# The causal mask of a fused four-layer attention kernel: on the four row tiles, 32 keys at a time, in place of products over the whole array

## The reference, cut to what matters

```python
scores = jnp.einsum('bhtd,bhsd->bhts', q, k) * q.shape[-1] ** (-0.5)
if causal:
    t, s = (scores.shape[-2], scores.shape[-1])
    mask = jnp.tril(jnp.ones((t, s), bool))
    scores = jnp.where(mask, scores, -jnp.inf)
p = jax.nn.softmax(scores, axis=-1)
o = jnp.einsum('bhts,bhsd->bhtd', p, v)
```

## Time and profile before

| | |
|---|---|
| time, median of 3 runs | 1405.27 us (1403.87 to 1406.78) |
| profiled execution: time, span | 1402.28 us, 1399.7 us |
| granted TensorE clock, mean | 0.996 of full |
| PE busy | 1343.6 us, 96% |
| PE weight loads (PEld) busy | 1144.9 us, 82% |
| DVE, ACT, POOL busy | 71%, 64%, 43% |

### The profile page before, as it was taken

The page is one execution under the profiler, slowest core; times in us unless marked ns, Lnnn a source line. Parts: engine busy times, 40 slices in busy tenths (PEclk is TensorE's granted clock), DMA queues, the critical chain, the costliest instruction groups (busy, mean ns, idle before and its releaser), DMA issues.

```text
span 1399.7 us, 45003 instructions
## 1 busy us (share of the span) xinstructions
PE 1343.6 (96%) x19500; PEld 1144.9 (82%) x19500; DVE 989.0 (71%) x1844; ACT 897.7 (64%) x1519; POOL 600.0 (43%) x767
## 2 busy tenths in 40 slices
PE   5899999999999999999999999999999999899997
PEld 5788888777887887787778888887999999688885
DVE  4777777787887777667766788788464445677675
ACT  4777677777767665666556776776443335767764
POOL 6644444676454732443334332225486665111100
PEclk9999999999999999999999999999999999999999
DMA  7211000101000100000000010000000000001000
GB/s 282 68 40 34 28 16 9 39 24 46 9 9 9 33 2 2 3 2 2 3 2 20 21 47 10 15 10 24 9 9 1 1 1 8 17 32 31 24 25 32
DMA packets 16316, 34.95 MB, mean 25 GB/s; under 512 B 1911, under 2 KB 7159, under 8 KB 15607
## 3 DMA queue, kind: packets, MB, share of 16 engines
q1 hardware_dynamic: 16119, 32.09, 7.2%
HBM read 27.89 MB, written 4.19 MB: 23 GB/s over the span
## 4 chain that ended last, share of the span: by engine, by line
PE 71%; DVE 14%; ACT 10%; issue 3%; DMA 1%; POOL 1%; SPq 0%; DVEq 0%; ACTq 0%; POOLq 0%
PE ps L712 9%; DVE s_nm L1098 9%; PE ps L777 8%; PE ps L739 6%; PE ps L805 6%; PE ps L791 6%; PE ps L657 5%; PE ps L604 5%; PE ps L756 5%; PE ps L629 4%; PE ps L616 4%; ACT s_PU L947 3%; PE ps L717 2%; PE ps L593 2%; PE ps L766 2%
## 5 line engine op out<-in xcount | busy, mean ns | idle before, releaser
L1098 DVE TENSOR_REDUCE s_nm<-ps 128x8 fp32r<-128x960 f32 (+1 forms) x352 | 395.5, 1167 | 108.6 <-PE ps L657 61.3
L947 ACT ACTIVATE s_PU<-ps 120x1024 f32<-120x1024 f32 (+1 forms) x288 | 279.5, 1025 | 103.8 <-PE ps L717 103.0
L712 PE MATMUL ps<-s_Qs,s_KH 32*120 32x256 f32 (+2 forms) x4608 | 184.4, 288 | 6.2 <-DVE s_nm L1098 2.9
L1222 POOL TENSOR_TENSOR s_xs<-s_xs,s_rowv 128x512 f32<-128x512 f32 x96 | 123.9, 1291 | 142.5 <-ACT s_nt L852 130.4
L1251 POOL TENSOR_SCALAR s_rs<-s_mv 128x2 f32<-128x2 f32 x96 | 21.7, 226 | 370.8 <-DVE s_mv L1135 364.9
L712 PEld LDWEIGHTS ps<-s_Qs,s_KH 32*120 32x120 f32 (+1 forms) x4608 | 150.6, 180 | 28.7 <-DVE s_nm L1098 6.1
L956 ACT ACTIVATE s_Os<-ps 128x512 f32<-128x512 f32 x160 | 94.5, 599 | 103.0 <-PE ps L739 55.8
L777 PE MATMUL ps<-s_W,s_oT 128*128 128x256 f32 x960 | 134.1, 289 | 3.5 <-DVE s_oT L1027 2.6
L604 PE MATMUL ps<-s_xT,s_W 128*128 128x256 f32 x960 | 135.3, 291 | 2.1 <-DVE s_xs L1119 1.4
L739 PE MATMUL ps<-s_PU,s_Vp 120*32 120x256 f32 x2048 | 129.1, 384 | 8.4 <-ACT s_PU L947 7.1
L777 PEld LDWEIGHTS ps<-s_W,s_oT 128*128 128x128 f32 x960 | 118.8, 188 | 13.9 <-issue 4.3
(11 more groups left out here) (100 smaller groups left out, 2592.4 us busy)
## 6 DMA issues: line engine op xcount, KB each, us to landing
s_cf<-ctx_t SPq DMA_DIRECT2D x32, 240.0 KB, 2.6
s_ws<-weights SPq DMA_DIRECT2D x28, 256.0 KB, 2.7
s_nt<-x_t SPq DMA_DIRECT2D x16, 256.0 KB, 2.8
s_xs<-x_nat SPq DMA_DIRECT2D x4, 1024.0 KB, 8.9
out<-s_xs SPq DMA_DIRECT2D x16, 256.0 KB, 2.0
s_rowv<-rows SPq DMA_DIRECT2D x6, 512.0 KB, 3.7
s_mi<-mask SPq DMA_DIRECT2D x8, 120.0 KB, 3.4
s_cst<-consts SPq DMA_DIRECT2D x1, 153.0 KB, 2.3
```

The lines of the kernel that those rows point to most:

```text
L712: e.matmul(banks[j][0:n, wide * x:wide * x + wide], kz[row[j], lk, g, c, k0:k0 + n], q[row[j], lq, g, qs_], start=(x == 0 and y_ == 0), st ...
L947: t = e.activation(P_of(i, k)[0:n, :, :], pair("B", i, k)[0:n, :, :], ACT.Exp, scale=0.25)
L1098: e.tensor_reduce(o, v, AX.X, ALU.max, negate=True).then_inc(sem["max"])
L1222: e.tensor_tensor(xs[:, b, :, :], xs[:, b, :, :], row2(layer, 0), ALU.add).then_inc(sem["pool"])
```

## The change

Each mask product over the whole array becomes four on every row tile, one for each block k of 32 queries. The stationary operand `who` (32x128, bf16) has ones that pick, for the queries of block k, the row of `gone` with the query's number in the block, and for the queries of earlier blocks the row 31, in which all is -2^100; `gone` (32x32, bf16, the same in each row tile) is the triangle of one block. The product is added on the 32 keys of block k, for all heads of the bank at once: 128 columns in unit 0 (four heads' slots of 32), 64 columns in units 1 and 2. So a unit has 16 mask matmuls in place of four, and `A` stays on the row tiles to its end.

`who` (128 KB) and `gone` (8 KB) are made on the host and come by two more DMAs in `mcols`; the constants are 64 KB smaller, and the two casts on DVE go. The plan is told that `A` of SELF ends on row tiles and takes 1.07 (before: 1.76 for unit 0 and 1.27 for the others). `STAY` goes from 0.006 to 0.236, and every entry of `WANT` but a few has another value, so that the order of all engines in all layers is another.

```diff
-WANT = dict(Xl=2.33, xT=-3, cT=-4, mi=-4, bo=(-1.38, -4.6, 0.82, 0.54, 4.02, -2.73), N=(0, 0, 7.36, 5.95, 4.46, 10.15),
+WANT = dict(Xl=-8.6, xT=-3, cT=-4, mi=-4, bo=(-0.05, 0.32, 4.13, 3.45, 8.95, -1.6), N=(0, 0, 6.16, 6.96, 8.36, 7.97),
...
+ROWMASK = True
 TURN = .19
-STAY = 0.006
+STAY = 0.236
...
-                array[0] = "whole" if name == "A" and layer_of(s.key[1]) == "SELF" else ARRAY.get(name, "whole")
+                array[0] = ARRAY.get(name, "whole")
...
-                    long=(1.76 if not u else 1.27) if self_ else .78 if layer == "L0" else None)
+                    long=1.07 if self_ else .78 if layer == "L0" else None)
...
-                w.wait_ge(sem["cst"], 4)
+                w.wait_ge(sem["d_msk"], 32)
...
-                    for j in range(4):
-                        t = e.matmul(banks[j].rearrange("p (r n) -> p r n", r=4), idb[:, :],
-                                     cbf[:, :].rearrange("p (o n) -> p o n", o=1).to_broadcast([128, 4, 128]), start=False, stop=True)
+                    off = [banks[j].rearrange("p (r b n) -> p r b n", r=4, b=4) for j in range(4)]
...
+                    off = [banks[j].rearrange("p (r b n) -> p r b n", r=2, b=8)[:, :, 4:8, :] for j in range(4)]
+
+                many = off[0].shape[1]
+                for k in range(4):
                     for j in range(4):
-                        t = e.matmul(banks[j].rearrange("p (c n) -> p c n", c=2)[:, :, 128:256], idb[:, :],
-                                     cbf[:, :].rearrange("p (o n) -> p o n", o=1).to_broadcast([128, 2, 128]), start=False, stop=True)
+                        t = e.matmul(off[j][:, :, k, :], who[row[j], k, :],
+                                     gone[row[j], :].rearrange("p (o n) -> p o n", o=1).to_broadcast([32, many, 32]),
+                                     start=False, stop=(k == 3))
                 t.then_inc(sem["A"])
...
-            e.tensor_copy(idb[:, :], ident[:, :]).then_inc(sem["cst"])
-            e.tensor_copy(cbf[:, :], caus[:, :]).then_inc(sem["cst"])
...
                 e.dma_start(mci[0:C, :], mask_t).then_inc(sem["d_mci"], 16)
+                e.dma_start(who[:, :, :].bitcast(u16), who_d).then_inc(sem["d_msk"], 16)
+                e.dma_start(gone[:, :].bitcast(u16), gone_d).then_inc(sem["d_msk"], 16)
...
+    q, row = np.arange(128)[None, None, :], part[:, None, None] % 32
+    block = np.arange(4)[None, :, None]
+    who = np.where(q // 32 == block, (row == q % 32) & (row < 31), (q // 32 < block) & (row == 31))
+    gone = np.where((np.arange(32)[None, :] > part[:, None] % 32) | (part[:, None] % 32 == 31), GONE, 0.0)
```

More of the change, by code:

```diff
@@ new lines @@
+WANT = dict(Xl=-8.6, xT=-3, cT=-4, mi=-4, bo=(-0.05, 0.32, 4.13, 3.45, 8.95, -1.6), N=(0, 0, 6.16, 6.96, 8.36, 7.97),
+            T=(0, -0.95, -0.09, -0.31, 0.05, -0.48), Q=(0.77, 0.4, 0.84, 0.53, 0, 0.96), Qh=(6.09, 3.57, 0.73, 1.06, 0, 0.55),
+            Ql=(4.86, 7.59, 5.47, 2.75, 0, 3.71), K=(0.69, 0.53, -0.61, -0.04, 0, 0.09), Kh=(8.28, 3.8, 10.87, 8.11, 0, 8.93),
+            Kl=(7.75, 11.88, 2.29, 5.3, 0, 6.15), K0=(-8.86, 4.8, 2.49, -0.38, 0, -5.31), V=(0.93, 1.19, 1.13, 1.09, 0, 1.14),
+            Ve=(6.09, 5.67, 5.17, 8.12, 0, 6.03), mf=5.42, A=(1.09, -0.04, -1.09, 0.86, 0, -0.96),
+            max=(0.19, -9.37, -4.86, -7.18, 0, 0.65), M=(-6.77, -4.88, -4.21, -4.16, 0, -9.54),
+            mTe=(5.28, 8.54, -0.91, -2.06, 0, 3.39), B=(-4.67, -7.08, -5.25, -3.98, 0, -6.3), exp=(-1.56, 3.06, 2.22, 3.8, 0, 4.84),
+            cap=-1.45, PV=(2.35, 1.54, 1.22, 1.96, 0, 2.46), PVe=(-4.89, -5.42, -3.15, 1.91, 0, 2.33),
+            ON=(3.22, 2.87, 3, 2.88, 0, -1.81), ONe=(1.73, 1.71, -1.22, -2.11, 0, 0.18), OT=(4.46, -4.46, 2.98, 2.5, 0, 3.93),
+            O=(-6.79, -9.94, -6.15, -1.26, 0, -4.83), y=(7.48, -1.3, 2.52, 6.31, 3.13, 1.93), st=(4.63, 7.35, 19.25, 15.89, 13.59, 0),
+            rs=(9.21, 4.54, 6.56, -2.53, 5.72, 0), ln=(5.45, 3.79, 0, 0, 0, 0), lng=(-7.5, -10.65, 0, 0, 0, 0), F1=-4.56, Fa=-4.54,
+            Fv=12.57, Hl=-14.14, F2=2.89, out=2.2, Th=(-5.93, -10.66, -3.47, -3.26, -7.11, -13.03),
+            Tl=(0, -1.48, 2.6, -2.01, 0.53, 4.69), OTh=(-7.18, -5.54, -13.03, -4.94, 0, -2.05),
+            OTl=(-4.46, 2.01, -4.88, -2.27, 0, -1.06), Ch=(5.54, 1.77, 0, -3.93, 0, -3.44), Cl=(-9.01, -5.12, 0, -5.24, 0, -7.35))
@@ L402, with program @@
 POOL_SEMS = ["pool"]
-DMA_SEMS = (["d_cst", "d_mci", "d_out"] + [f"d_x{k}" for k in range(4)] + [f"d_{n}{s}" for n in ("row", "mi", "nt") for s in range(2)]
+DMA_SEMS = (["d_cst", "d_mci", "d_msk", "d_out"] + [f"d_x{k}" for k in range(4)] + [f"d_{n}{s}" for n in ("row", "mi", "nt") for s in range(2)]
             + ["d_cf0"] + [f"d_ws{s}" for s in range(2)])
 N_CST = 16
-def program(nc, x_nat, x_t, ctx_t, mask, mask_t, weights, consts, rows, out):
+def program(nc, x_nat, x_t, ctx_t, mask, mask_t, weights, consts, who_d, gone_d, rows, out):
     f32, f32r, bf16, i32 = mybir.dt.float32, mybir.dt.float32r, mybir.dt.bfloat16, mybir.dt.int32
+    u16 = mybir.dt.uint16
     ALU, ACT, AX = mybir.AluOpType, mybir.ActivationFunctionType, mybir.AxisListType
@@ L444, in program @@
         rowv = [sb(f"rowv{i}", [128, 4, D]) for i in range(2)]
-        idb = sb("idb", [128, 128], bf16)
+        who = sb("who", [128, 4, 128], bf16)
         onb = sb("onb", [128, 128], bf16)
-        cbf = sb("cbf", [128, 128], bf16)
+        gone = sb("gone", [128, 32], bf16)
         pickr = sb("pickr", [128, 4], f32r)
@@ L450, in program @@
         gq = sb("gq", [128, 16])
-        cst = sb("cst", [128, 306])
-        ident, caus, hsel, pick, colv, c2 = (cst[:, a:b] for a, b in ((0, 128), (128, 256), (256, 258), (258, 262), (262, 282), (282, 306)))
+        cst = sb("cst", [128, 178])
+        ident, hsel, pick, colv, c2 = (cst[:, a:b] for a, b in ((0, 128), (128, 130), (130, 134), (134, 154), (154, 178)))
         ps = st.enter_context(nc.psum_tensor("ps", [128, 8, 512], f32))
@@ L641, in A @@
                 if layer == "L0":
-                    w.wait_ge(sem["cst"], 4)
+                    w.wait_ge(sem["cst"], 2)
                     w.wait_ge(sem["mf"], nth("mf", first))
@@ L943, in exp @@
                 if layer_of(i) == "L0":
-                    w.wait_ge(sem["cst"], 5)
+                    w.wait_ge(sem["cst"], 3)
                     t = e.activation(P_of(i, k)[0:n, :, :], pair("B", i, k)[0:n, :, :], ACT.Exp, scale=0.25, bias=mcol[0:n, i:i + 1])
@@ L1398, with bf16_bits @@
     part = np.arange(128)
-    causal = np.where(part[None, :] > part[:, None], GONE, 0.0).astype(np.float32)
+    q, row = np.arange(128)[None, None, :], part[:, None, None] % 32
+    block = np.arange(4)[None, :, None]
+    who = np.where(q // 32 == block, (row == q % 32) & (row < 31), (q // 32 < block) & (row == 31))
+    gone = np.where((np.arange(32)[None, :] > part[:, None] % 32) | (part[:, None] % 32 == 31), GONE, 0.0)
+    def bf16_bits(v):
+        return (np.ascontiguousarray(v, dtype=np.float32).view(np.uint32) >> 16).astype(np.uint16)
     headsel = np.stack([(part // 16) % 2 == 0, (part // 16) % 2 == 1], 1).astype(np.float32)
@@ L1406 @@
         "mask": g["mask_BxS2_if1"].reshape(B // 2, 2 * C), "mask_t": g["mask_BxS2_if1"].T,
-        "weights": weights, "consts": np.concatenate([np.eye(128, dtype=np.float32), causal, headsel, pick, cols], 1), "rows": rows,
+        "weights": weights, "consts": np.concatenate([np.eye(128, dtype=np.float32), headsel, pick, cols], 1),
+        "who": bf16_bits(who), "gone": bf16_bits(gone), "rows": rows,
     }
```

## The result

The changed kernel took 1396.39 us, the median of four runs (1395.82 to 1397.33), beside 1405.54 for the kernel before. The ratio is 0.9936, with a 95% interval of 0.9919 to 0.9954: 9.0 us faster, between 6.5 and 11.4. Measured again later on another chip it was 0.9957 (0.9945 to 0.9970), which is 6.4 us. The forecast was 1389.6 us with a range of 1377 to 1402. So the direction and the range were right, and the gain was forecast at 15.7 us, well above what came.

A forecast was written before the change was run, and what follows sets the result against it. The prediction took PE's instructions to bound an item of SELF. From 1405.27 us it took 13.1 us for the causal layer and 2.6 for the new order, 15.7 in all, with the start at 0: 1389.6 us, range 1377 to 1402.

The forecast's parts named there:

- The layer's 13.1 us: Causal layer SELF: net gain of 0.82 us for each of 16 items, 13.1 us in all.
- What goes: Per SELF item on PE: old mask products 2.09 us plus a weight-load stand of 0.21, 2.30 us removed.
- The 0.97 and twice 0.56: Old mask products per SELF item: 0.97 us for 512 columns, 0.56 each for units 1 and 2.
- What comes: Per SELF item on PE: 48 new row-tile matmuls add 1.32 us, bounded by 0.48 and 1.56.
- my lower bounds: New mask matmuls on row tiles: at least 15 ns with 128 columns and 7.6 ns with 64.
- the turn of 0.16 before `K`: After unit 0 in SELF: the turn to whole-array K is moved, not saved, adding 0.16 us per item.
- Rival (A): SELF: DVE's path takes over, wait for OTl grows 0.34 us, layer gains only 7.7 us; 1395.0 us, chance 0.17.
- The new order's 2.6 us: All layers: new due times and STAY save a quarter of a turn per attention item, 2.6 us.
- The start at 0: Kernel start: the two new mask DMAs cost 0, or 0.9 us if the assumed cover is gone.
- (B): Attention items: one turn fewer each, 10.4 us in place of 2.6; 1381.8 us, chance 0.17.
- (C): SELF: small matmuls cost 45 ns each and gain nothing, only the new order is left; 1402.7 us, chance 0.08.
- (D): Attention items outside SELF: passing over due stages starves PE, 28.8 us lost; 1421.0 us, chance 0.08.

The follow-up runs named there:

- The whole-array products in unit 2: Changed kernel with unit 2's mask added by 16 products of 64 columns over the whole array: 1397.50 us, 0.9956 of the kernel before.
- the doubling there: Changed kernel with the 16 mask products of unit 2 issued twice: 1396.37 us, 0.9946 of the kernel before.
- The products alone: New mask products with the order of the kernel before: 1395.33 us, 0.9940 of the kernel before.
- The kernel with both edits in the old order: New mask products in the old order, OTl ahead of Kl on DVE in SELF, mask DMAs behind the loads of x: 1389.45 us, 0.9902.
- the kernel with `OTl` first: New mask products in the old order, with OTl ahead of Kl on DVE: 1391.51 us, 0.9915 of the kernel before.
- the doubling in unit 1: Changed kernel with the 16 mask products of unit 1 issued twice: 1398.18 us, 0.9959 of the kernel before.

## Why the prediction was right in its range and too high in its gain

**The layer's 13.1 us** measured 16 x 0.76 = 12.2, but by errors that nearly cancel. *What goes* was too high by 0.21: the stand of the weight loads was counted beside distances from end to end, and unit 1 got shorter by 0.38 us, not by 0.60. The 0.97 and twice 0.56 stand. *What comes* was mis-sized the other way: by ends the 48 products add 0.25 + 2 x 0.17 = 0.59 us where I had 1.32. The line that I drew from 256 to 128 columns and on to 64 came from f32 rows. With bf16, 128 columns go at 0.25/16 = 15.6 ns where the f32 ones went at 28.8, and 64 columns at 8 ns: both are my lower bounds (15 and 7.6). The f32 weight load of 177 ns against 98 fits as the reason, and I named it and then set it aside; but the streamed operand changes its type too, and no run parts the two.

The page that I weighed, TensorEngine Tiling (Array Packing) of the Trainium skill, section Instruction Overhead, gives a matmul about 60 cycles of overhead, by my estimate 25 ns at 2.4 GHz. Read as a distance between any two matmuls, this doesn't hold here: the measurement decides, 8 ns. Read as a floor for one row tile it isn't contradicted, since each tile gets its next product only after 4 x 8 = 32 ns.

With 2.09 gone and 0.59 come, and the turn of 0.16 before `K` as I had it (no run measures it alone), PE's own saving is 2.09 - 0.59 - 0.16 = 1.34 us for an item, 21.4 us in all. Only 0.76 arrived. Where 0.58 went:

- Rival (A), with its mechanism as written, at 0.56 - 0.17 = 0.39 us where it had 0.34. PE is done with unit 2 that much earlier, and the path of the maxima, `Kl` and `OTl` is as long as before. The saving is turned into a wait of `PV` for the first maximum, which (A) had not named, rather than of `O` for `OTl`. The whole-array products in unit 2, the doubling there and the two lengths of 6.68 us show it.
- The remaining 0.19 lies at unit 0. From its start to the start of unit 1 it was 645.84 to 649.12 = 3.28 us before and is 643.53 to 646.44 = 2.91 now, 0.37 less where 0.97 - 0.25 - 0.16 = 0.56 could have gone. `K` now stands for ACT's exponential, its weight loads 4.9 us in 16 items. That this wait is the cause is read from the chain; no run took it away.

The prediction's step that failed is therefore the sentence that an item of SELF takes as long as PE's instructions take: 0.58 of the 1.34 us that went from PE came back as waits. PE at 98.7% busy before showed that it had next to no idle time then; it did not show that idle time wouldn't come in its place. I gave (A) 0.17.

**The new order's 2.6 us.** Wrong in sign: 4.1 us slower with the old products, and by the traces some 3.4 us slower behind SELF with either. I valued it at a quarter turn for an item. In the planned orders PE has 607 turns of kind before and after, the old mask's not counted: the larger `STAY` did not lower their number.

**The start at 0.** The bound of 0.9 was about right in size (1.0 to 1.1 us by the traces) and the value wrong: the second input was not covered.

**What is left.** The products alone gain 11.5 us between the `O` of item 29 and that of item 45, and the time fell by 7.3. Its profiled execution, laid beside the kernel before in the same order, shows where the rest went. The first `O` comes 5.4 us later, the kernel before shown second:

```profile
60.37 1.69 PE L782 MATMUL ps<-s_W,s_oT 128*128 128x256 f32 x12
```

```profile
54.93 1.69 PE L777 MATMUL ps<-s_W,s_oT 128*128 128x256 f32 x12
```

The distance stays at 5.4 to 5.6 us until SELF. Some of it is TensorE's clock (columns as above, the granted clock behind the five engines), first that kernel, then the one before:

```profile
30.00:40.00 10.00, 7.27 (x78) 6.37 (x82) 4.04 (x7) 5.25 (x11) 9.19 (x8) 0.54 0.26 71
...
960.00:970.00 10.00, 8.70 (x132) 6.61 (x130) 8.41 (x16) 6.16 (x10) 8.78 (x10) 0.81 0.01 2
```

```profile
30.00:40.00 10.00, 8.42 (x168) 5.95 (x166) 8.13 (x10) 7.28 (x11) 8.59 (x7) 0.93 0.42 117
...
960.00:970.00 10.00, 9.11 (x93) 7.91 (x92) 9.20 (x21) 7.77 (x16) 7.54 (x6) 1.00 0.01 2
```

At the start the half clock, 1.2 of 2.4 GHz, came behind a wait of PE for ACT in both (4.9 us, and 4.5 before) and stayed longer in the first. Behind SELF the kernel is 5.9 to 6.0 us ahead until the `O` of item 61 and 3.5 at the next one; in between lie the stretch shown and the ten us after it, with 0.81 and 0.85 where the kernel before has full clock. At the last `O` it is 2.6 ahead. The kernel with both edits in the old order has full clock there, and keeps its lead of 14.6 us (14.3 at the last `O`).

This profiled execution was the longest of the five (1399.69 us; the others 1392.8 to 1395.4), so it overstates the loss: with the same start, the kernel with `OTl` first had its first `O` only 2.1 us later than the kernel before, at 57.03 us. So in this profile the loss lies at the start and, with the low clock beside it, behind SELF. How much each is worth in a median run isn't measured, nor why the clock falls there.

Rivals (B) and (C) did not occur: the turns stayed as many, and the small products are cheap. (D) did not in its size of 28.8 us; the new order's loss behind SELF is 3.4, and which waits make it up is not shown.

## What to carry to other kernels

A unit of work is worth its own length only if nothing that runs beside it ends last. Before counting an engine's instructions as the gain, take the chain through one item, mark each piece that belongs to another engine, and ask of each removed instruction whether it lies on the chain or beside such a piece; here the mask of unit 2 lay beside DVE's maxima, and its shortening was worth nothing, and a swap of two neighbours in DVE's queue was then worth about 4 us. And when a small matmul's price is bounded from larger ones, ask first whether a row with the same operand type is among them: here the f32 rows gave 26.9 ns where 8 were measured.

## What the runs showed of the hardware that I had not expected

Matmuls on four row tiles with bf16 operands and 64 columns end at a distance of 8 ns (16 more of them in 0.13 us, by the doubling in unit 1), while the 128-column f32 ones go at 28.8 ns. Sixteen of 64 columns over the whole array, in unit 2, take 0.57 us up to the start of `PV`, turns included; on row tiles PE needed 0.31 for the same distance (0.59 less the wait of 0.28). A 128 KB load in front of the first inputs, 0.9 us of queue time, made ACT's copy of the second input start 2.5 us later than before (at 12.20 against 9.66 us), of which about 1 us reached the last `O` in the profiled execution.
